# PSUM banks dealt 3 and 3: three for transposed states and W_x products, three for the other tiles

## The reference

```python
proj = hidden_states @ W_in.T                  # 1024 -> 2 x 2048
x, gate = (proj[..., :D_IN], proj[..., D_IN:])
x = silu(causal_conv_of_4_taps(x) + conv_b)
ts, Bm, Cm = split(x @ W_x.T, 64, 16, 16)      # each then rms-normed
dt = softplus(ts @ W_dt.T + b_dt)
# for each token t, 2048 channels d, 16 states n:
state = state * exp(dt_t * A) + (dt_t * u_t) * B_t
y = sum over n of state * C_t
y = (y + x * D) * silu(gate)
out = y @ W_out.T                              # 2048 -> 1024
```

## Time and profile before

| | us |
|---|---|
| median of 3 runs | 3092.49 |
| lowest and highest | 3089.86, 3093.56 |
| profiled execution, its own time | 3095.74 |
| its span | 3093.7 |

### The profile page before, as it was taken

How to read it: one execution, slowest core, us unless ns; L and a number is a source line. 1 busy time by engine, 2 the same in 40 slices (tenths; PEclk the granted TensorE clock), 3 DMA queues, 4 the chain that set the end, 5 groups by cost and what they waited for, 6 DMA issues and landing times.

```text
span 3093.7 us, 34749 instructions
## 1 busy us (share of the span) xinstructions
PE 2757.5 (89%) x10928; PEld 1560.5 (50%) x10928; DVE 2602.0 (84%) x3602; ACT 1657.8 (54%) x2766; POOL 1848.4 (60%) x820
## 2 busy tenths in 40 slices
PE   8968899999989999998999887888878999999996
PEld 4535555555545555554555454554434555555553
DVE  2359998999999999999999999999945777787775
ACT  2346555565655656555565654655514555555553
POOL 1158787777878787786877887888821221222221
PEclk9988899999999999999999998889979999999998
DMA  5442323424252342424333322322121211111110
GB/s 173 130 104 79 107 82 91 144 83 134 79 157 84 103 136 82 132 84 153 89 98 100 96 84 90 119 84 72 48 69 35 89 54 61 61 54 54 61 61 21
DMA packets 132873, 281.28 MB, mean 91 GB/s; under 512 B 12528, under 2 KB 12656, under 8 KB 132224
## 3 DMA queue, kind: packets, MB, share of 16 engines
q1 hardware_dynamic: 132736, 279.59, 30.1%
HBM read 245.86 MB, written 33.69 MB: 90 GB/s over the span
## 4 chain that ended last, share of the span: by engine, by line
PE 49%; DVE 37%; issue 10%; ACT 2%; DMA 1%; POOL 0%; DVEq 0%; SPq 0%; ACTq 0%; POOLq 0%
DVE arena L1159 20%; PE banks L434 14%; DVE arena L1174 8%; PE banks L458 7%; PE banks L511 6%; PE banks L599 4%; PE banks L642 4%; PE banks L555 3%; PE banks L580 3%; PE banks L471 2%; PE banks L610 2%; DVE arena L1115 2%; PE banks L570 2%; DVE banks L1266 1%; DVE rbuf L1187 1%
## 5 line engine op out<-in xcount | busy, mean ns | idle before, releaser
L1159 DVE TENSOR_TENSOR_SCAN arena<-banks,arena 128x512 f32<-128x512 f32 x1024 | 1191.5, 1205 | 11.4 <-POOL arena L1085 11.1
L1085 POOL TENSOR_TENSOR arena<-arena 128x2048 f32<-128x2048 f32 x256 | 1161.7, 4538 | 58.4 <-PE banks L511 58.3
L937 ACT ACTIVATE banks<-arena,a_sb 128x508 f32<-128x508 f32 x1024 | 700.3, 684 | 822.5 <-DVE arena L1159 822.5
L434 PE MATMUL banks<-arena 128*128 128x512 f32 x2048 | 957.2, 605 | 20.2 <-DMA arena<-in_xT 8.2
L511 PEld LDWEIGHTS banks<-ident,arena 128*128 128x128 f32 x4096 | 501.1, 147 | 404.3 <-issue 226.0
L511 PE MATMUL banks<-ident,arena 128*128 128x128 f32 x4096 | 580.8, 286 | 126.6 <-DVE arena L1174 103.2
L1174 DVE SCALAR_TENSOR_TENSOR arena<-banks,cg,arena 128x512 f32<-128x512 f32 x720 | 511.0, 737 | 92.8 <-PE banks L511 91.4
L434 PEld LDWEIGHTS banks<-arena 128*128 128x128 f32 x2048 | 372.7, 195 | 371.9 <-issue 354.8
L458 PE MATMUL banks<-arena 128*128 128x512 f32 x1024 | 497.0, 621 | 46.5 <-DVE arena L1115 22.4
L1042 POOL TENSOR_TENSOR arena<-arena 128x512 f32<-128x512 f32 x240 | 305.1, 1271 | 360.2 <-ACT arena L781 356.6
L1096 POOL TENSOR_TENSOR arena<-arena 128x512 f32<-128x512 f32 x128 | 141.2, 1103 | 465.7 <-DVE arena L1322 465.7
(11 more groups left out here) (131 smaller groups left out, 2769.6 us busy)
## 6 DMA issues: line engine op xcount, KB each, us to landing
arena<-b_scratch SPq DMA_DIRECT2D x128, 512.0 KB, 5.2
arena<-in_WinX SPq DMA_DIRECT2D x128, 256.0 KB, 2.8
arena<-in_WinZ SPq DMA_DIRECT2D x128, 256.0 KB, 2.8
arena<-in_WoutT SPq DMA_DIRECT2D x32, 1024.0 KB, 5.8
u_scratch<-arena SPq DMA_DIRECT2D x64, 256.0 KB, 5.3
arena<-u_scratch SPq DMA_DIRECT2D x16, 1024.0 KB, 9.6
arena<-x_scratch SPq DMA_DIRECT2D x32, 512.0 KB, 3.4
arena<-in_xT SPq DMA_DIRECT2D x14, 1024.0 KB, 8.0
```

Source lines behind the costliest of these rows:

```text
L434: last = nc.tensor.matmul(home(kind, i), wr[w % 2][:, k, :], x[:, k, :], start=(k == 0), stop=(k == KC - 1))
L937: nc.scalar.activation(by_seq(bank(i % 2))[:, :, 1:SEQ], by_seq(dt[s % 2][:, i, :])[:, :, 1:SEQ], ACT.Exp, scale=a_sb[:, QD * q + i, n:n + ...
L1085: nc.gpsimd.tensor_tensor(hb[n % 4].rearrange("p (i t) -> p i t", i=QD), dtu, brep[n // 2 % 4][:, n % 2:n % 2 + 1, :].broadcast_to([P, QD, ...
L1159: nc.vector.tensor_tensor_scan(h, bank(i % 2), h, 0.0, ALU.mult, ALU.add)\
```

## The change

The turns, the W_x products and the transposed rows now share banks 2 to 4 in a list of their own, TURNS, and each waits only until the entry three before it has been read. The explicit waits around `pe_ssm` and `pe_rows` go. X, Z, D, O and Y tiles have banks 5 to 7, and `pe_room` looks three jobs back. ORDER, SIZES and the lists of the O sums and taps stay. dt of D0 to D3 moves on DVE from n = 5, 6, 8, 10 to 4, 6, 7, 10 (q = 3: from 6, 8, 10, 11 to 6, 7, 9, 11), and the chains for dt and the gate on ACT are moved to fit. Nothing of the computation changes.

```diff
+def turns():
+    found = [("S", p) for p in range(DT // 2)] + [("R", 0), ("S", DT // 2)]
+    for s in range(NS):
+        for n in range(N):
+            found += [("T", GB * (N * s + n) + b) for b in range(GB)]
+            if n == 1 and (has_x(s - 1) or s == 0):
+                found.append(("S", (LEAD + QD * s) // 2 - 1))
+            if n == 4 and s % NQ == NQ - 1 and s + 1 < NS:
+                found.append(("R", s // NQ + 1))
+            if n == 11 and has_x(s):
+                found.append(("S", (LEAD + QD * s) // 2))
+    return found
+TURNS = turns()
+SPOT = {j: k for k, j in enumerate(TURNS)}
...
         def home(kind, i):
-            return bank(4 + PLACE[kind, i] % 4)
+            return bank(5 + PLACE[kind, i] % 3)
+
+        def spot(kind, i):
+            return bank(2 + SPOT[kind, i] % 3)
...
             k = PLACE[kind, i]
-            if k >= 4:
-                kind, i = JOBS[k - 4]
+            if k >= 3:
+                kind, i = JOBS[k - 3]
                 pe.wait_ge(S[FREED[kind]], i + 1)
+
+        def pe_turn_room(pe, kind, i):
+
+            k = SPOT[kind, i]
+            if k < 3:
+                return
+            kind, i = TURNS[k - 3]
+            if kind == "S":
+                pe.wait_ge(S["ss_added"], i + 1)
+            elif kind == "R":
+                pe.wait_ge(S["bt_rows"], i + 1)
+            elif i % GB == OWN:
+                pe.wait_ge(S["part_ok"], i // GB + 1)
+            else:
+                pe.wait_ge(S["acc_ok"], OWN * (i // GB) + i % GB + 1)
...
                 def turn(b):
 
-                    if b == 1:
-                        after(pe, "part_ok", U)
-                    else:
-                        after(pe, "acc_ok", OWN * U + (0, 0, 1, 2)[b])
+                    pe_turn_room(pe, "T", GB * U + b)
...
                 pe.wait_ge(S["scan_ok"], QD * (U + 1))
-                if n == 2 and (has_x(s - 1) or s == 0):
-                    pe.wait_ge(S["ss_added"], (LEAD + QD * s) // 2)
-                if n == 5 and q == NQ - 1 and s + 1 < NS:
-                    pe.wait_ge(S["bt_rows"], g + 2)
-                if n == 12 and has_x(s):
-                    pe.wait_ge(S["ss_added"], (LEAD + QD * s) // 2 + 1)
...
                 if n == 1 and (has_x(s - 1) or s == 0):
-                    pe.wait_ge(S["acc_ok"], OWN * (U + 1))
                     pe_ssm(pe, (LEAD + QD * s) // 2 - 1)
...
-                if e == 29:
+                if e == 25:
                     act_dt_abs(act, D)
+                if e == 26:
                     act_dt_exp(act, D)
-                if e == 30:
+                if e == 28:
                     act_dt_ln(act, D)
...
                 for i in range(QD):
-                    if n == ((6, 8, 10, 11) if late else (5, 6, 8, 10))[i]:
+                    if n == ((6, 7, 9, 11) if late else (4, 6, 7, 10))[i]:
                         dve_dt(dve, D + i)
```

More of the change, by code:

```diff
@@ L465, in pe_ssm @@
             pe.wait_ge(S["u_ok"], 2 * p + 2)
-            after(pe, "ss_added", p)
+            pe_turn_room(pe, "S", p)
             if p == 0:
@@ L470, in pe_ssm @@
                 for m in (2 * p, 2 * p + 1):
-                    last = nc.tensor.matmul(bank(2)[:, b * SS:(b + 1) * SS], cv[m % 3][:, b * P:(b + 1) * P],
+                    last = nc.tensor.matmul(spot("S", p)[:, b * SS:(b + 1) * SS], cv[m % 3][:, b * P:(b + 1) * P],
                                             wxT[:, m % DT, :], start=(m == 2 * p), stop=(m == 2 * p + 1))
@@ L477, in pe_rows @@
             pe.wait_ge(S["ss_normed"], 3 * GB * (g + 1))
+            pe_turn_room(pe, "R", g)
             for b in range(GB):
-                last = nc.tensor.transpose(bank(2)[0:SS, b * P:(b + 1) * P], ssn[:, b, :], ident[:, :])
+                last = nc.tensor.transpose(spot("R", g)[0:SS, b * P:(b + 1) * P], ssn[:, b, :], ident[:, :])
             last.then_inc(S["bt_mm"], 1)
@@ L504, in turn @@
                 def turn(b):
-                    if b == 1:
-                        after(pe, "part_ok", U)
-                    else:
-                        after(pe, "acc_ok", OWN * U + (0, 0, 1, 2)[b])
+                    pe_turn_room(pe, "T", GB * U + b)
                     for i in range(QD):
-                        last = nc.tensor.transpose(bank(2 + b % 2)[:, i * P:(i + 1) * P],
+                        last = nc.tensor.transpose(spot("T", GB * U + b)[:, i * P:(i + 1) * P],
                                                    hb[n % 4][:, i * GT + b * P:i * GT + (b + 1) * P],
@@ L780, in act_part @@
                 dst = part[:, n % 2, :]
-            nc.scalar.activation(dst, bank(3), ACT.Identity, scale=cg[:, OWN, n:n + 1])\
+            nc.scalar.activation(dst, spot("T", GB * (N * s + n) + OWN), ACT.Identity, scale=cg[:, OWN, n:n + 1])\
                 .then_inc(S["part_ok"], 1)
@@ L838, in act_between @@
                     act_dt_ln(act, D + 1)
-                if e == 37:
+                if e == 36:
                     act_z_copy(act, Z + 2)
                     act_z_exp(act, Z + 2)
+                if e == 37:
+                    act_dt_abs(act, D + 2)
+                    act_dt_exp(act, D + 2)
                 if e == 38:
-                    act_dt_abs(act, D + 2)
-                if e == 40:
-                    act_dt_exp(act, D + 2)
+                    act_dt_ln(act, D + 2)
                 if e == 41:
-                    act_dt_ln(act, D + 2)
                     act_z_ln(act, Z + 2)
@@ L876, in act_between @@
                     act_z_copy(act, Z + 1)
-                if e == 37:
                     act_z_exp(act, Z + 1)
+                if more and e == 37:
+                    act_dt_abs(act, D + 1)
+                    act_dt_exp(act, D + 1)
+                if e == 38:
+                    if more:
+                        act_dt_ln(act, D + 1)
                     act_z_ln(act, Z + 1)
-                if e == 38:
+                if e == 40:
                     act_z_sig(act, Z + 1)
[L882 to L886, removed]
                 if mine and e == 42:
                     act_base(act, X + 1)
+                if more and e == 42:
+                    act_dt_abs(act, D + 2)
                 if more and e == 44:
-                    act_dt_abs(act, D + 2)
+                    act_dt_exp(act, D + 2)
+                    act_dt_ln(act, D + 2)
                 if mine and e == 45:
@@ L1123, in dve_ss_add @@
             if p % (DT // 2) == 0:
-                last = nc.vector.tensor_copy(v, bank(2)[:, 0:GB * SS])
+                last = nc.vector.tensor_copy(v, spot("S", p)[:, 0:GB * SS])
             else:
                 dve.wait_ge(S["ss_added"], p)
-                last = nc.vector.tensor_tensor(v, v, bank(2)[:, 0:GB * SS], ALU.add)
+                last = nc.vector.tensor_tensor(v, v, spot("S", p)[:, 0:GB * SS], ALU.add)
             last.then_inc(S["ss_added"], 1)
@@ L1144, in dve_rows @@
             after(dve, "b_stored", 16 * g)
-            nc.vector.tensor_copy(tsb[0:SS, :], bank(2)[0:SS, :]).then_inc(S["bt_rows"], 1)
+            nc.vector.tensor_copy(tsb[0:SS, :], spot("R", g)[0:SS, :]).then_inc(S["bt_rows"], 1)
         def dve_dt(dve, j):
@@ L1170, in dve_acc @@
                     dve.wait_ge(S["cg_ok"], s // NQ + 1)
-                last = nc.vector.tensor_scalar(acc[:, b, :], bank(2 + b % 2), c, None, ALU.mult)
+                last = nc.vector.tensor_scalar(acc[:, b, :], spot("T", GB * (N * s + n) + b), c, None, ALU.mult)
             else:
                 dve.wait_ge(S["acc_ok"], k - OWN + 1)
-                last = nc.vector.scalar_tensor_tensor(acc[:, b, :], bank(2 + b % 2), c, acc[:, b, :],
+                last = nc.vector.scalar_tensor_tensor(acc[:, b, :], spot("T", GB * (N * s + n) + b), c, acc[:, b, :],
                                                       ALU.mult, ALU.add)
```

7 lines of the change are left out of this document (removed).

## The result

The changed kernel takes 3146.12 us (median of 4 runs, 3143.92 to 3149.59), beside 3093.02 for the kernel before: ratio 1.0168, interval 1.0155 to 1.0181. It is 53 us slower; forecast were 30, with 3084 to 3148 as range.

What follows compares the result with a forecast made beforehand. VectorE was taken to set the pace, idling when a filler tile with a late bank holds back the next transposes. Terms: -53 + 77.3 + 6 = +30 us, so 3122 us; bounds gave 3098 to 3150, the range was set to 3084 to 3148.

Steps and rivals of the forecast that it cites:

- 1 W_x products: At n = 2 and 3, steps 1 to 11: DVE's waits behind these products mostly go; 17 us won, bounds 9 and 29.
- 2 O3 after D2: At n = 9: O3 now needs O0's bank, long free, so 11 waits, together 22.8 us, all go.
- 3 Z3, rows, n = 14: Z3 behind D2 in every fourth step, the transposed rows, and n = 14: waits go, together 13 us won.
- 4 X2 after O2 or D2: Before the n = 10 transposes: X2's four units wait for a late bank in ten steps; 37.7 us lost, the largest term.
- 5 D2, O0 at n = 6: End of n = 6: D2 follows X1, O0 follows D1, two units behind the taps instead of one; 7.9 us lost.
- 6 steps 3 and 7: In these two steps X1 waits for D0's bank and O2 for X0's; 7.3 us lost.
- 7 O6 after X3: End of n = 14: O6 follows X3 where it followed Z3, 1.06 us in ten steps; 10.6 us lost.
- 9 logarithm of D0: At n = 4: DVE waits for ScalarE's logarithm, moved to slot 28, before the dt sum; 8.6 us lost.
- the clock: PE's granted clock falls at the ten waits before X2; 6 us lost, bounds 0 and 20.
- Rival A: Faster by decoupling: a third bank lets PE run ahead past late rooms, X2 starting without a wait; 3056 us, chance 0.13.
- Rival B: Even: gains and losses cancel, with no clock loss and some losses hidden; 3086 or 3092 us, chance 0.12.
- Rival C: Much slower: each new wait over 2.5 us lowers the clock, 2 us more at 18 places; 3150 to 3160 us, chance 0.07.

Runs made afterwards that it cites:

- e2: Changed kernel with turns, W_x products and rows back on their old banks and waits, three banks kept for X, Z, O, D, Y: 3191.23 us, ratio 1.0319.
- e3: Changed kernel with the logarithm for dt of D0 on ScalarE one slot earlier, 27 for 28, in steps with q < 3: 3146.54 us, ratio 1.0174.
- e4: Kernel before with only the moved dt and gate operations, banks and waits as before: 3092.80 us, ratio 0.9997.
- e6: Changed kernel with the last transposes of n = 6 and n = 9 made six times in steps with X tiles: 3118.99 us, ratio 1.0089.
- e10: Kernel before with only the moved dt and gate operations, plus the last transposes of n = 1 made five times in steps 1 to 11: 3071.22 us, ratio 0.9931.

## Why the prediction was right, and where its size was off

The mechanism held at every place. The size is another matter: 3146 lies 2 us inside the upper end of the range, and 23 us beyond the forecast. The terms, as sums of DVE's waits at each place in the traces of before and after (us):

| step of the prediction | forecast | measured |
|---|---|---|
| 1 W_x products | -17 | -25, and +2 at n = 1 |
| 2 O3 after D2 | -23 | -23 |
| 3 Z3, rows, n = 14 | -13 | -12 |
| 4 X2 after O2 or D2 | +37.7 | +49.8 |
| 5 D2, O0 at n = 6 | +7.9 | +14.8 |
| 6 steps 3 and 7 | +7.3 | +7.2 |
| 7 O6 after X3 | +10.6 | +26.4 |
| 8 O0 without X | +5.2 | +5.6 |
| 9 logarithm of D0 | +8.6 | +9.9 |
| the clock | +6 | in the terms 4, 5, 7 |
| sum | +30 | +56 |

The scan stage ends 54.2 us later, 2330.9 for 2276.7 us, so the table accounts for it within 2 us. The first term gained 6 us more than I gave it, since Z0's lateness left the product unhindered and cost DVE some 2 us at n = 1.

The step that was mis-sized is the term for the clock, 6 us. The terms 4, 5 and 7 exceed their price by units by 12.1, 6.9 and 15.8, together 35 us. The 1.1 us a place that I read at the O0 place was near enough: 12.1 us at ten places of X2 are 1.2 each, and 35 us at 28 places the same. What was wrong is where I charged it: at the ten waits before X2 alone, while the eight waits before D2 and the ten before O6, 3.1 to 4.8 us of idle PE each, most of them longer than X2's 3.33, got nothing. Then I halved it because the waits before the W_x products go, though term 1 had booked the 8 us of these slow cases already. The range held because term 1 erred by 6 us the other way and because its upper end was wide; a part of that is luck. The earlier trace rows also hold less than I read in them: 0.67 over 3 us and 0.84 over 6 us are each about 2 us at half speed, not 3.

For terms 4 and 5 the clock is shown as the cause: kept busy, they fell to their prices by units, and n = 7 even below its 17.3 us of before, where the clock had been lost there too. For term 7 it is read from the trace only: behind O6's wait in step 4 of the changed kernel PEclk is 0.59 (866.10 to 869.30). The price of 1.06 us appears in step 4 of the kept-busy kernel (at 858.27), 2.3 to 3.7 in most others after the same 3.69 us of wait.

Rival A failed where it was to decide: X2 waits, 3.33 us each time. The turn part, which A is about, does win 45 us (e2), but the filler part loses 98. Rival B had the clock loss at nothing, and fails with it; its sum was also off, as the terms 6, 7 and 9 make 26.5 us and not 18, so B was 3078 us, outside the range. Rival C is nearest in total (3150 to 3160): its 36 us for the clock are the 35 measured, though at 2 us for 18 places and not 1.2 for 28, and its condition fails, since the 3.33 us waits of X2 lowered the clock in three steps of eight only. Of the signs I named, all came but one: DVE's L1199 waits 137.7 us, not less than 80, step 4 lasts 136.8 us (said: 135 to 136), L507 no longer waits, and D2 waits for L1140, but L494 waits for L1175 in three steps only (12 to 14). In the steps with X tiles and q < 3, D2, one job ahead of O0, waits for the taps first and runs until D1's dt sum is done.

The Trainium skill (TensorE: Matmul & The Clock Gate, HAM oscillation — how this bites in real kernels) describes a matmul kernel in which each wait for data lets the clock fall so that every next piece starts slow. This case's trace agrees in part, with waits for PSUM banks in place of transfers: the clock is 0.53 behind D2's wait, but 1.00 behind X2's in step 4, so here not every next piece starts slow.

## What to carry to other kernels

When an engine works in written order through two interleaved streams, ask of each shared buffer not how many there are but at which place of the order its next user stands: one sum moved by one state was worth 37 us, one swap of two tiles 36 us, and neither needed a bank. Price a late buffer as the time from its release to the restart of the engine that sets the pace: a fixed part (0.87 us here) plus the work that stands between, less what that engine still has to do meanwhile. Price that work at both clocks, at every wait and not only at the largest; the length of a wait alone did not tell which applies. In the kernel before, W_x products behind the same 2.23 us of idle time took 2.02 us in step 3 and 3.73 in step 2, and here X2's units took 3.70 or 6.72 us. A measured zero may be two effects (e3, e4): look at the trace before dropping the edit.

## What was not expected of the hardware

Idle work before a wait paid: 420 more transposes on TensorE saved 27 us (e6), and 176 saved 22 (e10). Equal waits are not followed by equal clocks: after the same 3.33 us of idle time four units took 3.70 us in step 4 and 6.72 in step 1 of the changed kernel, and 6.44 in step 4 of e3, whose only difference is one ScalarE operation. What decides between the two was not settled here; it makes edits of 10 us readable only beside the trace.
